# Expert products ahead of their side work on TensorE, and first query and key tiles ahead of the last outputs' turn: a two-layer kernel on one core

## What is computed

```
h = _layernorm(x, axis=-1) * (1 + cb) + sb
x = x + gb * _L0_ffn_ref(h, ...)          # experts, the first place of the change
...
h = _layernorm(x, axis=-1) * (1 + ca) + sa
x = x + ga * _L1_attn_ref(h, ...)          # its last outputs: the second place
h = _layernorm(x, axis=-1) * (1 + cb) + sb
x = x + gb * _L1_ffn_ref(h, ...)           # six blocks of local attention
```

## Time and profile before

| | us |
|---|---|
| median of 3 runs (lowest, highest) | 2232.56 (2232.53, 2233.05) |
| the profiled execution | 2237.4 |
| its span | 2235.6 |
| TensorE busy in the span | 2033.6 (91%) |
| VectorE busy | 1806.9 (81%) |
| ScalarE busy | 1578.8 (71%) |
| GpSimd busy | 1165.9 (52%) |

### The profile page before, as it was taken

How to read it: one execution, slowest core, us unless ns; L and a number is a source line. 1 busy time by engine, 2 the same in 40 slices (tenths; PEclk the granted TensorE clock), 3 DMA queues, 4 the chain that set the end, 5 groups by cost and what they waited for, 6 DMA issues and landing times.

```text
span 2235.6 us, 82638 instructions
## 1 busy us (share of the span) xinstructions
PE 2033.6 (91%) x34491; PEld 1473.6 (66%) x34491; DVE 1806.9 (81%) x3751; ACT 1578.8 (71%) x3031; POOL 1165.9 (52%) x1413
## 2 busy tenths in 40 slices
PE   6888899987789998999999999999999999999997
PEld 4666564444567776777767777777667777677764
DVE  6778775467778888898888888888889888888884
ACT  4666753345557778877878777777777787877773
POOL 1111110000277666767666767676676676766761
PEclk9999999998889999999999999999999999999999
DMA  4000000000122223322232223222233222332221
GB/s 111 2 2 2 2 1 0 1 1 1 48 75 63 67 60 85 85 69 67 74 85 74 68 60 101 69 71 71 57 91 81 72 70 57 92 80 66 76 57 39
DMA packets 94676, 125.83 MB, mean 56 GB/s; under 512 B 27484, under 2 KB 42466, under 8 KB 94306
## 3 DMA queue, kind: packets, MB, share of 16 engines
q1 hardware_dynamic: 94306, 120.54, 20.7%
HBM read 21.91 MB, written 1.05 MB: 10 GB/s over the span
## 4 chain that ended last, share of the span: by engine, by line
PE 59%; DVE 10%; ACT 5%; issue 4%; POOL 1%; SPq 0%; DMA 0%; POOLq 0%; ACTq 0%; DVEq 0%
PE oo L565 16%; PE pj L565 15%; PE tr L568 13%; PE sc L565 12%; ACT arena L1891 3%; PE tr L565 2%; DVE arena L1699 2%; DVE xn L1292 2%; DVE arena L1701 1%; DVE arena L1720 1%; DVE arena L1722 1%; PE oo L568 1%; ACT xcur L1891 1%; ACT sc L1891 1%; DVE arena L1707 1%
## 5 line engine op out<-in xcount | busy, mean ns | idle before, releaser
L2309 POOL TENSOR_TENSOR arena<-arena 128x1024 f32<-128x1024 f32 x192 | 457.1, 2381 | 349.6 <-DVE arena L1701 349.6
L1891 ACT ACTIVATE arena<-tr 128x512 f32<-128x512 f32 (+2 forms) x874 | 462.2, 571 | 161.3 <-PE tr L568 112.3
L1891 ACT ACTIVATE arena<-pj 128x512 f32<-128x512 f32 x576 | 341.6, 599 | 191.1 <-PE pj L565 154.8
L568 PE MATMUL tr<-ident,arena 128*128 128x128 f32 x2978 | 429.6, 279 | 28.9 <-DMA beta<-in_L_attn_betas 9.9
L568 PEld LDWEIGHTS tr<-ident,arena 128*128 128x128 f32 x2978 | 342.3, 142 | 116.7 <-issue 51.8
L1891 ACT ACTIVATE arena<-arena 128x16 f32<-128x16 f32 (+6 forms) x808 | 355.3, 453 | 57.5 <-DVE arena L1460 26.7
L2327 POOL TENSOR_TENSOR arena<-arena 128x1024 f32<-128x1024 f32 x192 | 366.1, 1907 | 23.2 <-POOL arena L2320 0.9
L1699 DVE TENSOR_TENSOR arena<-pj,rtab 128x512 f32<-128x512 f32 x384 | 259.9, 677 | 30.1 <-ACT arena L1891 28.4
L565 PE MATMUL oo<-slab,arena 64*32 64x64 f32 (+1 forms) x12416 | 231.3, 229 | 42.2 <-issue 27.8
L1701 DVE TENSOR_TENSOR arena<-pj,rtab 128x512 f32<-128x512 f32 x384 | 261.5, 681 | 0.0
L1707 DVE TENSOR_REDUCE arena<-arena 128x8 f32<-128x512 f32 x384 | 255.8, 677 | 0.0
(11 more groups left out here) (288 smaller groups left out, 3816.4 us busy)
## 6 DMA issues: line engine op xcount, KB each, us to landing
slab<-arena SPq DMA_DIRECT2D x576, 128.0 KB, 2.4
slab<-arena SPq DMA_DIRECT2D x336, 64.0 KB, 2.0
wqkv<-in_L_ffn_Wqkv SPq DMA_DIRECT2D x18, 512.0 KB, 4.6
wo<-in_L_ffn_Wo SPq DMA_DIRECT2D x6, 512.0 KB, 4.3
w<-in_L_ffn_W SPq DMA_DIRECT2D x6, 341.0 KB
YT<-in_L_attn_x SPq DMA_DIRECT2D x4, 256.0 KB, 4.1
arena<-in_L_ffn_W SPq DMA_DIRECT2D x1, 1024.0 KB
out_x<-arena SPq DMA_DIRECT2D x4, 256.0 KB, 2.2
```

Of the source, the lines that this page charges most:

```text
L568: return nc.tensor.transpose(o, i, ident[0:i.shape[0], 0:i.shape[0]])
L1891: return nc.scalar.activation(o, i, f, **k)
L2309: p_.tensor_tensor(r_, r_, rb[:, k, :], ALU.add).then_inc(sum_ok, 1)
```

## The change

In `experts`, `up(j)` stands ahead of `beside(b, n)` from step 1 on. In slot 0 the first key tile (`project(0, 0, 2)`) and its square stand ahead of `out_turn(1, 3)` and of the copy that belongs to it; the projection of that output stands behind the second key tile instead of behind the first. On VectorE `mix(3)` stands ahead of the second sum of squares. On GpSimd `power` of D 3 in slot 1 stands ahead of the second `add_parts`. Nothing is added and nothing is left out.

```
                 for j in range(NE * B):
                     b, n = divmod(j, NE)
                     if j >= 1:
+                        up(j)
                         beside(b, n)
-                        up(j)
                     spread(j)
...
                     queries(0)
                     queries(1)
-                    crossing(g, 1)
+                    if g > 0:
+                        crossing(g, 1)
...
                     project(g, t, 2)
-                    crossing(g, 2)
+                    if g == 0:
+                        crossing(g, 1)
                 if d_:
                     probs()
                 if new:
                     project(g, t, 3)
+                    crossing(g, 2)
...
                 if new:
+                    if g == 0:
+                        crossing(g, 2)
                     lengths(g, 1)
-                    crossing(g, 2)
+                    if g > 0:
+                        crossing(g, 2)
...
                     square(g, 1)
-                    crossing(g, 1)
+                    if g > 0:
+                        crossing(g, 1)
...
                     square(g, 2)
+                    if g == 0:
+                        crossing(g, 1)
...
+                    if g == 1:
+                        power(LNA, NORM_AT["D", 3])
                     add_parts(g, t, 1)
-                    if g < 2:
-                        power(LNA, NORM_AT["D", 2 + g])
+                    if g == 0:
+                        power(LNA, NORM_AT["D", 2])
```

## The result

| | before | the change |
|---|---|---|
| median of 4 runs each, us | 2232.55 (2232.21 to 2233.05) | 2209.72 (2205.85 to 2211.34) |
| ratio | | 0.9899, 95% interval 0.9883 to 0.9914 |
| the profiled execution, us | 2237.4 | 2208.49 |
| its span, us | 2235.6 | 2206.7 |

The account below looks back on a forecast made before the run. TensorE, busy 91% of the span, was taken as the bound, so only its waits and lower clock could pay. Experts 17.6 and crossing 5.2 summed to 22.8 us gained, giving 2209.8 us from 2232.6, range 2204 to 2218.

Parts of the forecast that it names:

- the step that I thought covered by 0.7 us: Experts, n = 6: ScalarE's relus behind norm_end end later, but the multiplication is done at 5.7 against 6.4; costs nothing.
- the rival of the loops: Twelve experts waits are closed loops that up lengthens by 1.72 us each, so slower, 2248.0 us; chance 0.03.
- the size of each wait in the experts: TensorE's waits ahead of side work and the last down, each idle time less 0.24 us: 16.7 us in all.
- the one at 465.02: Experts, a late stack product's load waiting for low; the stack products' waits were 1.58, 2.52, 0.21 and 1.25 us.
- Step 1: Experts: the last heads' turn comes 1.72 us later and delays the first down; loss 0.4 us, bounds 0 and 1.0.
- The row that spoke for the loops: Experts: stack products at 459.37 and 465.02 lie 5.65 us apart, against 4.73 for a step and two loads.
- The clock in the experts, 1.9 us: Window 450 to 460 at granted clock 0.83, slowing step 28; 1.9 us taken as gained, bounds 0 and 1.9.
- my lower bound (14.5 - 0.4 = 14.1): Experts: 14.5 us if waits are hidden only up to up's 1.72 and the multiplication gains nothing, less step 1's 0.4.
- Slot 0: Crossing: VectorE rotates the second key tile at 607.65 instead of 610.68, the chain behind follows; 3.0 us gained, bounds 0.6 and 4.1.
- the lower bound 0.6: Slot 0: smallest gain, 0.6 us, if only mix(3) ahead of the second sum of squares counts.
- Slots 1 and 2: Crossing: earlier power of D 3 saves GpSimd 1.3 us and a TensorE wait of 0.90; 2.2 us together, bounds 1.3 and 3.4.
- rival 5: With fewer waits the clock stays high in the crossing too, 3 to 5 us more gained, 2206 us; chance 0.12.

Follow-up runs that it names:

- crossing only: The whole changed crossing with the experts as before, against the kernel before: 2226.27 us, ratio 0.9974.
- slot 0 only: Only the change's parts in slot 0, power of D 3 left behind the second addition, against the kernel before: 2228.01 us, ratio 0.9991.
- with fillers: Kernel before plus five products that nothing reads, three at the end of slot 0, two in slot 2: slot 3 at 55.10 us, before 56.93.
- with the mix alone: Kernel before with only VectorE's mix(3) in slot 0 moved ahead of the lengths of the key half: 2228.31 us in one run.
- power only: Only GpSimd's power of D 3 moved ahead of its second addition in slot 1, against the kernel before: 2224.82 us, ratio 0.9978.
- first three: Kernel before with up ahead of beside only for sequences 0 to 2, crossing as before: 2223.68 us in one run, experts 161.42.
- more moved: The change plus, in slot 0, the turn into D 2, an output addition and power of D 2 moved later: 2207.34 us, ratio 0.9879 to the kernel before.

## Why the prediction was right, and where it was not

- **The bound was right.** All of the gain is TensorE's standing still or running at the lower clock. No new wait of TensorE on the relus came up, the step that I thought covered by 0.7 us cost nothing measurable, and the rival of the loops (2248.0) is out.
- **The step that failed is the size of each wait in the experts.** I took idle time of the load less 0.24, and behind products of 512 columns it is less 0.67. With that for all twelve 16.7 becomes 11.8, and less 0.5 at step 1 and 0.2 that the load at 447.13 still waits, 11.1. Measured are 12.4. The lengths of the steps say where the 1.3 more lie: eleven waits were 0.3 to 0.4 shorter than I forecast, 3.9 in all, and not 0.43 each, and the one at 465.02 was 0.48 and not 0.21. That makes 13.1 us of waits. 0.3 of the largest are left in step 29 (5.06 us, its work 4.73), steps 10 and 18 together got 0.2 shorter, and step 1 lost 0.5. The sum is 12.5, and 12.4 was measured. Why the loads overstate a wait by 0.3 in one place and 0.4 in another stays open.
- **Step 1** lost 0.5 us (forecast 0.4).
- **The row that spoke for the loops was misread.** The 5.65 us from 459.37 to 465.02 stood against 4.73, which leaves out the turn of that step (0.43); against 5.17 only the wait of 0.48 is left.
- **The clock in the experts, 1.9 us, happened in the profile that I read, and not always.** It was worth 1.74 in that profile and 1.5 to 1.6 in the others. The profiles of the same order in other kernels had it five times (before, crossing only, slot 0 only, and the two further down with fillers and with the mix alone, 167.0 to 167.2 us) and two times not (power only and, with its fourth sequence unchanged, first three). None of the seven profiles with `up`, or half of it, ahead in the fourth sequence had it. So the new order does take the fall away, but a kernel of before has it only in some executions, and I should have taken a part of it. The rule that I weighed, from the Trainium skill ("TensorE: Matmul & The Clock Gate", Part 1), is that the low clock is the default and activity releases it; the 1.9 did go, as by that rule, but the same idle times gave a fall in one execution and none in another. The Trainium skill, in the same place, calls the number of slow products at the start of a kernel "run-variable"; it says so of the start only, and here a fall in the middle of the kernel varied as well.
- **Experts in sum:** 12.4 + 1.7 = 14.1, forecast 17.6. Without the clock even my lower bound (14.5 - 0.4 = 14.1) was above the 12.4 measured, since both bounds were made from the same misread waits.
- **Slot 0 was right by its own steps**: 3.1 for 3.0, the second key tile's rotation 3.08 earlier (forecast 3.0), and the lower bound 0.6 measured by itself at 0.6.
- **Slots 1 and 2: the waits were right, 2.3 for 2.2, but a term was missing,** 2.5 us of clock, of which the added products show 1.8 by themselves. It was rival 5's mechanism, which I had as a rival with 3 to 5 us. The profile showed it: the transposes at 635.83 take 1.75 us, and I used that row for its wait alone.
- **The sum.** 14.1 and 8.0 (slot 4) make 22.1, near 22.8 because an error of 3.5 too much and one of 2.8 too little offset each other. That the median fell by 22.8 to the tenth is luck: medians of the change were 2209.7 and 2208.3, those of before 2232.6, 2231.7, 2233.9 and 2229.2. Differences on one chip are 22.8 and 20.9.

## What to carry to other kernels

A weight load that has come late shows a longer idle time than TensorE has: take the wait from the spacing of equal steps, or, less exactly, from the idle time of the load less all that it has in a step without a wait and behind the same kind of product, the lead over its product included. When work that is ready is put ahead of work that waits, each wait shrinks by the length of what was moved and no further; half as long a piece gives the short waits whole. Where the lower clock shows in a row that you cite for a wait, cost it there too, and ask for a second profile before counting on a single fall of the clock.

## What the runs showed of the hardware

- The clock's fall in the experts came in five of seven profiles of one order of the fourth sequence (0.83 in 450 to 460 in the first, later by some microseconds in the others) and cost 1.5 to 1.7 us each time; it came in none of seven with the new one.
- Unread products added ahead of a wait can shorten a stretch: 4.6 us of them brought slot 3 of the kernel before 1.8 us forward. In the version with more moved such products gave 0.1 us there.
- Four of VectorE's multiplications of 128x128 took 2.66 us beside GpSimd's addition of 128x1024, and 0.89 behind it.
- An undisturbed stretch of 153.12 us repeated in five profiles to 0.01 us, while 29 runs of the kernel before went from 2224.5 to 2238.2; much of the scatter is in the slots, where a block of 16 took 261.4 to 266.5 us with the same code.
